# A projection stage whose normalisation moves ahead of its evictions, and attention's preparations in one program block

## The reference, cut to what matters

```python
def _layernorm(x, axis=-1, eps=1e-05):
    m = jnp.mean(x, axis=axis, keepdims=True)
    v = jnp.var(x, axis=axis, keepdims=True)
    return (x - m) / jnp.sqrt(v + eps)
...
qkv = hidden_states @ W_attn + b_attn
q, k, v = jnp.split(qkv, 3, axis=-1)
...
scores = jnp.einsum('bhqd,bhkd->bhqk', q, k) / jnp.sqrt(jnp.float32(D))
```

## Time and profile before

| | |
|---|---|
| median of 3 runs | 1362.17 us (1360.82 to 1364.11) |
| profiled execution | 1361.62 us |
| its span, first to last instruction | 1359.6 us |
| granted TensorE clock, mean over the span | 0.954 |
| PE busy, over the span | 1229.7 us (90%) |
| the projection stage with attention's preparations, to PE's first product of attention | the first 82.1 us of the span |

### The profile page before, as it was taken

The page is one execution under the profiler, slowest core; times in us unless marked ns, Lnnn a source line. Parts: engine busy times, 40 slices in busy tenths (PEclk is TensorE's granted clock), DMA queues, the critical chain, the costliest instruction groups (busy, mean ns, idle before and its releaser), DMA issues. The chain is left out here.

```text
span 1359.6 us, 32622 instructions
## 1 busy us (share of the span) xinstructions
PE 1229.7 (90%) x13048; PEld 714.2 (53%) x13080; DVE 862.5 (63%) x1742; ACT 571.0 (42%) x854; POOL 248.2 (18%) x444
## 2 busy tenths in 40 slices
PE   5769999999999999878999968995999999969998
PEld 2433333333333333254677644442888888857775
DVE  6367878888888888345433364897576666643432
ACT  2314777777777776823133214652211111112221
POOL 4220010000001001040277500233222111000000
PEclk9867999999999999998999988997999999979999
DMA  4310112211111220051143320000200000000000
GB/s 127 54 23 4 29 28 40 41 28 27 28 27 29 40 39 3 3 160 62 32 162 101 119 79 0 0 0 5 76 4 4 4 4 3 4 2 0 16 16 31
DMA packets 33836, 49.47 MB, mean 36 GB/s; under 512 B 11995, under 2 KB 22331, under 8 KB 32955
## 3 DMA queue, kind: packets, MB, share of 16 engines
q1 hardware_dynamic: 29211, 36.55, 12.1%
q0 software_dynamic: 3744, 10.23, 2.4%
q10 hardware_dynamic: 768, 1.05, 0.2%
HBM read 23.63 MB, written 9.31 MB: 24 GB/s over the span
## 5 line engine op out<-in xcount | busy, mean ns | idle before, releaser
L664 DVE TENSOR_REDUCE at_block_max<-at_p_ring 128x4 f32<-128x512 f32 x576 | 367.7, 686 | 76.3 <-PE at_p_ring L570 42.2
L641 ACT ACTIVATE at_probs<-at_p_score,abias 128x1024 f32<-128x1024 f32 (+2 forms) x320 | 318.8, 1029 | 123.2 <-PE at_p_score L600 69.0
L570 PE MATMUL at_p_ring<-kt,qt 64*128 64x128 bf16 (+3 forms) x1152 | 187.2, 284 | 18.5 <-PEq L727 7.4
L615 PE MATMUL at_p_out<-at_probs,at_vs 128*32 128x512 f32 (+3 forms) x1536 | 164.5, 500 | 0.4 <-ACT at_probs L641 0.4
L594 PE MATMUL at_p_score<-qt,kt 64*128 64x512 bf16 (+3 forms) x768 | 146.2, 332 | 5.7 <-ACT at_probs L641 4.8
L570 PEld LDWEIGHTS at_p_ring<-kt,qt 64*128 64x128 bf16 x1152 | 69.9, 95 | 130.4 <-DVE at_block_max L664 86.6
L707 POOL TENSOR_TENSOR at_shift<-shift,at_row_max 128x16 f32<-128x16 f32 x32 | 7.1, 221 | 423.2 <-DVE at_row_max L670 423.2
L594 PEld LDWEIGHTS at_p_score<-qt,kt 64*128 64x128 bf16 x768 | 38.4, 94 | 85.7 <-ACT at_probs L641 55.2
L2055 ACT COPY rc_ta<-rc_bank 128x256 f32<-128x256 f32 x32 | 10.3, 375 | 148.9 <-PE rc_bank L1826 148.9
L2184 PE MATMUL fi_p_in<-fi_xt,w_in 128*128 128x512 f32 x128 | 64.2, 626 | 0.7 <-ACT fi_xt L2221 0.7
L600 PE MATMUL at_p_score<-anticausal,ident 128*128 128x128 bf16 (+1 forms) x384 | 62.3, 244 | 0.0
(11 more groups left out here) (334 smaller groups left out, 2153.9 us busy)
## 6 DMA issues: line engine op xcount, KB each, us to landing
qt<-qparts SPq DMA_DIRECT2D x96, 64.0 KB, 2.4
kt<-kparts SPq DMA_DIRECT2D x96, 64.0 KB, 2.5
rows<-moe_chosen SPq DMA_DIRECT2D x4, 1024.0 KB, 4.8
w_routed<-in_w_routed_dram SPq DMA_DIRECT2D x1, 2816.0 KB
x<-in_x_dram SPq DMA_DIRECT2D x4, 512.0 KB, 8.4
moe_table<-rows SPq DMA_DIRECT2D x4, 512.0 KB, 2.7
out_dram<-x SPq DMA_DIRECT2D x4, 512.0 KB, 2.9
w_down<-in_w_down_dram SPq DMA_DIRECT2D x1, 1408.0 KB
```

Of the source, the lines that this page charges most:

```text
L570: mm = pe.matmul(bank[:, col:col + nb * P], qt[nxt][h * ROWS:(h + 1) * ROWS, pair, t * P:(t + 1) * P], kt[nxt][h * ROWS:(h + 1) * ROWS, pa ...
L615: mm = pe.matmul(p_out[32 * h:32 * h + 32, left(k):QC], vs[(now - e[2]) % BUFS][:, key, h, :], probs[g % PROBS][:, h % 2, at:at + w], star ...
L641: act.activation(probs[g % PROBS][:, :, 0:len(pairs) * w], p_score[g % 2][:, :, 0:len(pairs) * w], ACT.Exp, bias=abias[:, c * TPB + key:c ...
L664: dve.tensor_reduce(dst, src, AX.X, ALU.max).then_inc(s["fill_used"], 1)
```

## The change

- DVE's list: each chunk is normalised right behind its moments, chunk 0 before chunk 1's statistics, chunk 2 before the first eviction; `normalise(3)` stands between `evict(0)` and `evict(1)`. The additions for v become a function `evict_values(n)` and stand behind the evictions of q and k of two chunks.
- ACT's list: `split(1)` comes ahead of `take(2)`.
- PE's list: `turn(2)` comes ahead of `values(0)`.
- POOL waits for the second chunk's `xn` before its two casts.
- The three casts of the masks go from DVE and a block of their own to ACT in the block of the memsets, and one of three pairs of POOL's memsets (`vs[1]`) goes to DVE.

```diff
+
+                def evict_values(n):
                     for j in range(2):
                         dve.wait_ge(v_ready, 2 * n + j + 1)
...
                 statistics(0)
                 moments(0)
+                normalise(0)
                 statistics(1)
-                normalise(0)
                 moments(1)
-                statistics(2)
                 normalise(1)
                 dve.wait_ge(w_loaded, 3 * 16)
                 dve.tensor_scalar(w[:, :, 0:E], w[:, :, 0:E], HD ** -0.5, None, ALU.mult).then_inc(scaled, 1)
                 dve.tensor_scalar(b_turned[:, 0::2], b_turned[:, 0::2], HD ** -0.5, None, ALU.mult).then_inc(scaled, 1)
+                statistics(2)
                 moments(2)
+                normalise(2)
                 statistics(3)
                 moments(3)
                 dve.wait_ge(scaled, 2)
                 evict(0)
-                normalise(2)
+                normalise(3)
                 evict(1)
-                normalise(3)
+                evict_values(0)
+                evict_values(1)
                 evict(2)
                 evict(3)
+                evict_values(2)
+                evict_values(3)
...
                 split(0)
+                split(1)
                 take(2)
-                split(1)
                 take(3)
...
                 pool.wait_ge(edge_loaded, 2 * 16)
+                pool.wait_ge(xn_ready, 2)
                 pool.tensor_copy(krows16[:, :, :], krows[:, :].unsqueeze(1).to_broadcast([2 * PLACES, 2, S])
...
                 queries_and_keys(1)
+                turn(2)
                 values(0)
-                turn(2)
                 values(1)
...
         with nc.Block() as block:
+            @block.scalar
+            def _(act):
+                act.copy(ident16[:, :], ident[:, :])
+                act.copy(causal16[:, :, :], causal[:, :].unsqueeze(1).to_broadcast([P, QC // P, P]))
+                act.copy(anticausal16[:, :, :], anticausal[:, :].unsqueeze(1).to_broadcast([P, 2, P]))
+
             @block.vector
             def _(dve):
                 dve.memset(block_max[:, :, :], NEG)
+                dve.memset(vs[1][:, :, :, HD + 1:32], 0.0)
+                dve.memset(vs[1][:, :, :, HD:HD + 1], 1.0)
 
             @block.gpsimd
             def _(pool):
                 pool.memset(shift16[:, :, :, :, :], 0.0)
-                for i in range(BUFS):
+                for i in (0, 2):
...
-                with nc.Block() as block:
-                    @block.vector
-                    def _(dve):
-                        dve.tensor_copy(ident16[:, :], ident[:, :])
-                        dve.tensor_copy(causal16[:, :, :], causal[:, :].unsqueeze(1).to_broadcast([P, QC // P, P]))
-                        dve.tensor_copy(anticausal16[:, :, :], anticausal[:, :].unsqueeze(1).to_broadcast([P, 2, P]))
```

More of the change, by code:

```diff
@@ L483, in ring_place, with attention_phase @@
     return ring_count(by_scalar, u) + (1 + sum(in_ring(e) and (e[0] == "shift") == by_scalar for e in ev[:n]))
-def attention_phase(nc, ident, ident16, causal16, anticausal16, abias, shift0, qparts, kparts, v, qrows16, qt, kt,
+def attention_phase(nc, ident, causal, anticausal, ident16, causal16, anticausal16, abias, shift0, qparts, kparts, v, qrows16, qt, kt,
                     stack_loaded, attn):
@@ L2390, in two_blocks_program @@
                                 chunks, weights, start_loaded, later)
-                with nc.Block() as block:
-                    @block.vector
-                    def _(dve):
-                        dve.tensor_copy(ident16[:, :], ident[:, :])
-                        dve.tensor_copy(causal16[:, :, :], causal[:, :].unsqueeze(1).to_broadcast([P, QC // P, P]))
-                        dve.tensor_copy(anticausal16[:, :, :], anticausal[:, :].unsqueeze(1).to_broadcast([P, 2, P]))
-                attention_phase(nc, ident, ident16, causal16, anticausal16, abias, shift0, qparts, kparts, v, qrows16,
+                attention_phase(nc, ident, causal, anticausal, ident16, causal16, anticausal16, abias, shift0, qparts, kparts, v, qrows16,
                                 qt, kt, stack_loaded, attn)
```

## The result

| | median, us | lowest to highest | ratio to before |
|---|---|---|---|
| before | 1361.49 | 1359.58 to 1364.11, 6 runs | |
| changed | 1344.47 | 1340.99 to 1346.43, 6 runs | 0.9873 [0.9856, 0.9889] |

By the medians the change makes the kernel 17.0 us faster; 16.6 was forecast. The profiled execution of the changed kernel took 1343.78 us, 17.8 less than that of before, with 1341.9 between its first and its last instruction.

A forecast was written before the change was run, and what follows sets the result against it. PE's list plus its waits for DVE set the first stage: 4.4 - 2.2 + 10.1 + 2.5 = 14.8, plus 1.8 for preparations, 16.6 us off 1361.62; median forecast 1345.6, range for 8 in 10 1338.5 to 1349.

The forecast's parts named there:

- start: Up to the first q and k product: products start at 16.0 instead of 20.47 us, gain 4.4.
- new wait: PE waits for DVE's first eviction before the second chunk's products: loss 2.2 us, bounds 0.4 and 2.5.
- middle and tail: Rest of the first stage: PE's two gaps and slow clock go, 10.1 us; shorter end behind the last product, 2.5.
- stage end: The first stage, which ended at 77.90 us, was to end at 63.1, a gain of 14.8.
- preparations: Between stage end and attention's first product: casts moved and memsets shared, 2.44 us instead of 4.19, gain 1.8.
- attention: Clock at attention's start still falls soon behind the start: value 0, bounds -1.5 and +7 us.
- SP's list: SP's 39 DMA issues, 24.8 us, end at 61.1 to 62.5, before the stage's 63.1; costs nothing, up to 1 if late.
- The upper way of reckoning: In the new wait, POOL's casts block DVE's small operations too: eviction done at 25.85, stall bound 2.5 us.
- The rival in which the clock survives: PE's higher clock lasts into attention, giving up to 7 us more, 1339 us in all; chance 0.15.

The follow-up runs named there:

- e1: Changed kernel without POOL's wait for the second chunk's `xn`, so its two casts start at once; 1346.11 us, ratio 0.9892.
- e2: Changed kernel with POOL's two casts moved to ACT behind `take(0)`; 1342.33 us, ratio 0.9860.
- e4: Changed kernel with each chunk's value additions right behind its own q and k evictions on DVE again; 1354.99 us, ratio 0.9952.
- e9: Changed kernel with SP's 13 stack issues for attention's third unit moved from the first stage to attention's main block; 1344.55 us, ratio 0.9878.
- e3: Changed kernel with preparations as before: three mask casts on DVE in their own block, all memsets on POOL; 1348.38 us, ratio 0.9905.
- e6: Changed kernel with POOL's casts on ACT and ten extra PE transposes in the preparations' block; 1358.28 us, ratio 0.9959.
- e7: Changed kernel with four of the third unit's stack DMAs issued by ACT instead of SP; 1344.31 us, ratio 0.9881.
- e5: Changed kernel with ten extra PE transposes in the preparations' block, during the memsets; 1358.20 us, ratio 0.9975.
- e12: Changed kernel with its start as before: chunk 1's statistics ahead of chunk 0's normalisation, POOL's casts at once; 1345.18 us, ratio 0.9899.
- e11: Changed kernel with ten extra transposes at the very start of PE's list; 1358.28 us, ratio 0.9983.
- e8: Changed kernel with one extra 128x512 PE product behind each fill of attention's first unit, 36 in all; 1370.27 us, ratio 1.0063.

## Why the prediction was right, step by step

| step | forecast, us | measured, us | how |
|---|---|---|---|
| start | +4.4 | +4.1 | products at 16.36 instead of 20.47 |
| new wait | -2.2 (-0.4 to -2.5) | -1.8 | PE's row at 25.88 |
| middle and tail | +12.6 | +12.6 | no gaps, full pace, 0.73 behind the last product |
| stage end | 63.1 | 63.0 | DVE's and SP's last rows; 14.9 in all |
| preparations | +1.8 | +1.45 | 4.19 before, 65.75 - 63.01 = 2.74 now |
| attention | 0 (-1.5 to +7) | +0.6 up to the copy of unit 3 | copies 16.35, 16.59 and 16.96 earlier |
| sum | 16.6 | 17.0 | |

Each step came out in kind, but for SP's list. That the sum is off by only 0.4 is partly luck: start and preparations brought 0.3 us less each, the new wait cost 0.4 less, and the clock gave 0.6 that no step had forecast.

- **Start.** Right, but for 0.3: chunk 1's statistics waited for their data until 9.98, where 9.6 was taken, and all behind them came 0.3 to 0.4 later.
- **The new wait.** The upper way of reckoning was right in kind: small operations of DVE do stand still for POOL's casts. By that way chunk 2's root was to start at 19.35 and chunk 3's at 23.9, and they started at 19.51 and 23.99; the first eviction ended at 25.73, where 25.6 had been taken. The stall is 1.8 instead of 2.2 because PE came there 0.65 later than taken, after more half pace at its start. The runs show that this size is chance: with the same code it was 0.5 to 1.9 us, and what repeats is the 9.5 us from the first chunk's products to the second's (forecast: 16.0 to 25.6). The rule of the Trainium skill that had been set against the edit ("SBUF — State Buffer", "SBUF: two separate sides": a shared pair of ports held for a whole instruction, also by DVE operations with two inputs in SBUF while GpSimd reads SBUF) is what e1 shows with its 0.58 and 1.80, and e2 with its 0.16.
- **Middle and tail.** Right as a sum and in each row: no gap, transposes 0.93 shorter, products 1.89 shorter, and one addition (0.73 to the end) behind PE's last product instead of 3.16. `normalise(3)` met low parts (2.84 us instead of 1.38) and nobody waited. e4 shows that 8.4 us, most of this, rest on the values' evictions standing apart.
- **SP's list "costs nothing".** This step was wrong by 0.35 us. The list began at 37.73, the late end of the forecast, and ended at 63.00, 0.5 past it; and the border follows SP's last issue by 0.64 us where it follows DVE by 0.29. The forecast had taken 0.34 for either. e9 shows it, and it is also what the preparations are short of their 1.8: against e3, whose border is set by SP too, they bring the full 1.8. ACT's three casts took 1.1 us and didn't stick out.
- **Attention's clock.** The fall came as expected. The value was 0, and it gave 0.6: the clock came back 37.3 us behind the first product instead of 38.6, unit 1 took 31.8 instead of 32.1, and unit 2 took 29.1 instead of 29.5. Among nine kernels the length of unit 1 follows that time at about 0.5 us for each us (37.2 to 37.6: 31.4 to 31.8; 38.6: 32.1; 39.7: 32.5; 39.9 and 40.1: 33.0 and 33.1). Unit 0 isn't free of the clock either: where it fell 1.7 us behind the first product (e9) or 2.7 behind it (e6), this unit took 27.6 and 27.4 instead of 28.4. The edit isn't shown to be what shortened the slow time: e7 has the changed kernel's order on PE, DVE and POOL, and there the clock came back after 40.1. The rival in which the clock survives fell in this trace, and in e5 and e6 the clock fell behind shorter gaps too.
- **The rest.** From the copy of unit 3 to the last one (before 527.35, now 510.39) the distance stays 16.96. The profiled executions lie 0.7 us further apart than that, where short falls of the clock come in later stages; what sets these, I couldn't settle. They differ between profiles whose code there is the same: behind the last copy e12 gains 2.7 us on the changed kernel, and e3 loses 1.5.

## What to carry to other kernels

An earlier start is worth only what the next wait leaves of it: reckon the feeding engine's list to the end of its first eviction, and on to the border, not only to the first product (e12: 3.0 us became 1.9). An operation that waits for a late engine must not stand in a list ahead of work that this engine's next input needs (e4: 8.4 us up to attention for the places of two pairs of additions). And a few instructions more can cost more far behind than at their own place (e11: 0.6 us at attention's start, 14 in all), so an experiment that adds some needs its own control. A stall in one profile is one draw: compare the start behind it over several kernels with the same code before you put a price on it (9.5 us in eight kernels, with stalls of 0.5 to 1.9).

## What the runs showed of the hardware, unexpected

- The pauses of 2.5 to 3 us in attention's loop that come with ten more instructions on PE, each behind two loads of instructions close together, and the wide spread of such kernels (e11: 1347.5 to 1364.6 over ten runs).
- A PE that is busy without a gap for 44 us at a granted clock of 0.50 (e8).
- The profile's clock can't be read at the very start. The trace's records of it begin at 19.8 us in e2 and at 17.7 in the changed kernel, and for stretches before that the view prints 1.00. PE's first products run at half pace there. The weight loads of e2 show it:

```profile
18.05 0.34 PEld L302 LDWEIGHTS qkv_p_qk<-qkv_xt,w_qkv 128*128 128x128 f32 x1 [0.52 <-issue]
18.90 0.34 PEld L302 LDWEIGHTS qkv_p_qk<-qkv_xt,w_qkv 128*128 128x128 f32 x1 [0.52 <-issue]
19.75 0.21 PEld L302 LDWEIGHTS qkv_p_qk<-qkv_xt,w_qkv 128*128 128x128 f32 x1 [0.52 <-issue]
20.20 0.19 PEld L302 LDWEIGHTS qkv_p_qk<-qkv_xt,w_qkv 128*128 128x128 f32 x1 [0.24 <-issue]
```

  They are 0.85 us apart until 19.75 and 0.43 to 0.45 after; in the changed kernel the pace doubled near 17.5, two us earlier. So the records begin where the pace doubles. Over the 14 kernels that is 1.2 to 4.1 us behind the first 128x512 product, and 1.2 to 4.0 among the eight with the same code up to there. What decides the moment is open; it is why e2 gained 1.03 us and not 1.82.
- Issues of DMAs on two queues at once took up to 1.37 us each instead of 0.6 (e7), and the border of a block comes 0.35 us later behind SP's last issue than behind DVE's or POOL's last operation (0.65 to 0.69 against 0.29 to 0.34).
